# A four-layer graph and attention kernel: a reordered prologue and an earlier first choice

## What is computed

```python
h = (x @ W.T).reshape(n, H, D)                       # the values
e_l = einsum('nhd,hd->nh', h, a_l); e_r = einsum('nhd,hd->nh', h, a_r)
logits = leaky_relu(e_l[:, None] + e_r[None, :], 0.2) + gate * einsum('ijf,hf->ijh', abs(curv_i - curv_j), Wc)
out = einsum('ijh,jhd->ihd', softmax(where(adj > 0, logits, -1e9), axis=1), h)
...
q = x @ Wq_pk; sim = q . pk_keys                     # 2 x 128 scores for each row and head
the 16 best of each half, their 256 sums, the 16 best of those: 16 rows of a table of 131072
k, v = softmax(scores) . keys_table[rows], values_table[rows]
out = causal attention of x @ Wq with k and v, @ Wo
```

## Time and profile before

| what | value |
|---|---|
| time, median of 3 executions | 4347.53 us (4346.95 to 4349.38) |
| profiled execution, its own time | 4337.04 us |
| span of the profiled execution | 4335.3 us |
| mean granted TensorE clock | 0.918 |
| busy: PE, DVE, ACT, POOL | 80%, 77%, 53%, 47% |

### The profile page before, as it was taken

One profiled execution on the slowest core, in us unless ns is written; L12 is line 12 of the kernel. 1 busy time (PEld: TensorE's weight loads), 2 busy tenths in 40 slices (PEclk: granted clock), 3 DMA queues, 4 the chain that ended last, 5 costly groups with the idle time before them and its releaser, 6 DMA issues. The chain is left out here.

```text
span 4335.3 us, 62381 instructions
## 1 busy us (share of the span) xinstructions
PE 3470.9 (80%) x19465; PEld 2679.8 (62%) x19592; DVE 3336.2 (77%) x10591; ACT 2284.3 (53%) x3657; POOL 2049.0 (47%) x2052
## 2 busy tenths in 40 slices
PE   6867777777778788888888989566888888888797
PEld 4645555555555565566666666445677777777575
DVE  2679889899898898898988989663877777777334
ACT  5645455555555555565555655222656666665232
POOL 0377777777777777777766767660000000000000
PEclk9988889999999999999999999777999999999799
DMA  2244444554555555555555556554000000000100
GB/s 75 61 128 118 133 139 134 146 153 141 156 149 162 168 170 174 170 179 176 180 180 184 189 168 205 171 181 160 1 1 1 1 1 1 1 1 1 41 0 10
DMA packets 187672, 477.90 MB, mean 110 GB/s; under 512 B 43933, under 2 KB 87137, under 8 KB 182881
## 3 DMA queue, kind: packets, MB, share of 16 engines
q0 software_dynamic: 98304, 268.57, 21.4%
q1 hardware_dynamic: 89052, 205.52, 14.0%
HBM read 447.57 MB, written 26.21 MB: 109 GB/s over the span
## 5 line engine op out<-in xcount | busy, mean ns | idle before, releaser
L508 POOL DMA_INDIRECT ck_ring<-in_tables,ck_rows x2048 | 2048.8, 1000 | 879.4 <-issue 751.3
L993 DVE SCALAR_TENSOR_TENSOR ck_part<-ck_ring,ck_norm_w,ck_part 128x256 f32<-128x256 f32 x1792 | 768.7, 475 | 62.5 <-DVE ck_rows L968 41.7
L567 PE MATMUL psV<-ck_vals,ck_probsT 128*128 128x128 f32 x4096 | 554.2, 284 | 112.3 <-ACT ck_probsT L742 105.8
L552 PE MATMUL psL<-ck_bias_rhs,ck_bias_w 110*128 110x512 f32 x1024 | 571.7, 641 | 87.0 <-ACT ck_bias_rhs L729 38.4
L567 PEld LDWEIGHTS psV<-ck_vals,ck_probsT 128*128 128x128 f32 x4096 | 501.8, 196 | 161.3 <-ACT ck_probsT L742 92.0
L1204 PE MATMUL psL<-ga_probsT,ga_vals 128*128 128x256 f32 x2048 | 528.1, 405 | 0.7 <-ACT ga_probsT L1301 0.7
L742 ACT COPY ck_probsT<-psT 128x512 f32<-128x512 f32 x512 | 281.3, 587 | 443.5 <-PE psT L559 439.1
L1204 PEld LDWEIGHTS psL<-ga_probsT,ga_vals 128*128 128x128 f32 x2048 | 398.7, 205 | 51.6 <-ACT ga_probsT L1301 0.9
L1191 PE MATMUL psT<-ident,ga_probs 128*128 128x128 f32 x2048 | 303.0, 283 | 153.8 <-ACT ga_probsT L1301 149.5
L1191 PEld LDWEIGHTS psT<-ident,ga_probs 128*128 128x128 f32 x2048 | 248.8, 146 | 204.4 <-issue 184.1
L1292 ACT ACTIVATE ga_probs<-ga_probs,ga_neg_mx 128x2048 f32<-128x2048 f32 x128 | 256.5, 2004 | 220.9 <-DVE ga_neg_mx L1352 220.5
(11 more groups left out here) (205 smaller groups left out, 5616.0 us busy)
## 6 DMA issues: line engine op xcount, KB each, us to landing
ck_ring<-in_tables,ck_rows POOLq DMA_INDIRECT x2048
ck_adj_raw<-in_adj SPq DMA_DIRECT2D x16, 1024.0 KB, 9.5
adj_scratch<-ck_adj_neg SPq DMA_DIRECT2D x16, 512.0 KB
values_scratch<-ck_values_tile SPq DMA_DIRECT2D x128, 64.0 KB, 1.7
keysT_scratch<-ck_keys_tile SPq DMA_DIRECT2D x128, 64.0 KB
ck_keysT<-keysT_scratch SPq DMA_DIRECT2D x8, 1024.0 KB
ck_values<-values_scratch SPq DMA_DIRECT2D x8, 1024.0 KB
ga_adj_neg<-adj_scratch SPq DMA_DIRECT2D x16, 512.0 KB, 11.9
```

The costliest lines, as they stand in the source:

```text
L508: pool.indirect_dma_start(ring[:, slot, :], None, ins["tables"], bass.IndirectOffsetOnAxis(rows[:, k, s:s + 1], axis=0)).then_inc(got[(u * ...
L552: last = nc.tensor.matmul(psL[:, c * CH:(c + 1) * CH], bias_w[:, :], bias_rhs[:, k % 2, c * CH:(c + 1) * CH], start=False, stop=True)
L567: last = nc.tensor.matmul(psV[:, k % 2, :], probsT[:, q % 2, s, :], vals[:, j, :], start=(j == 0), stop=(j == T - 1))
L993: done.append(c.did(nc.vector.scalar_tensor_tensor(part[:, s % 2, :], ring[:, slot, :], norm_w[:, s:s + 1], part[:, s % 2, :], ALU.mult, A ...
```

## The change

There are two parts, all in the one stage. In the prologue, SP issues the loads of L445 to L454 before it waits, and the wait for the right scores and the two transfers of them come last; its constant goes from 13 to 12. TensorE multiplies left and right scores before the values are multiplied the second time, and ScalarE copies in the same order, with the first difference put between the second and third copy of the values. VectorE makes the first mask before it picks the left scores. In the first unit with a choice (`opening`), the scores go ahead of the next logits on TensorE, their copy ahead of relu and difference on ScalarE, and the choice ahead of the next maximum on VectorE.

```diff
@@ SP
-                sp.wait_ge(prep_copied, 13)
-                for b in range(2):
-                    sp.dma_start(bias_rhs[KW:KB, b, :], er_rows[0:H, :]).then_inc(er8_in, 16)
                 sp.dma_start(wq[:, :, :], ins["Wq_pk"]).then_inc(keys_in, 16)
...
                 sp.dma_start(ahead[:, :], ins["c_ahead"][:, 0, 0:P]).then_inc(at_in, 16)
+                sp.wait_ge(prep_copied, 12)
+                for b in range(2):
+                    sp.dma_start(bias_rhs[KW:KB, b, :], er_rows[0:H, :]).then_inc(er8_in, 16)
@@ TensorE, prologue
+                pe.wait_ge(weights_ready, 2)
+                pe.wait_ge(prep_copied, 4)
+                for c in range(NC):
+                    nc.tensor.matmul(psL[...], al_w, hT[...], start=True, stop=True).then_inc(prep_mm, 1)
+                for c in range(NC):
+                    pe.wait_ge(prep_copied, 5 + c)
+                    nc.tensor.matmul(psL[...], ar_w, hT[...], start=True, stop=True).then_inc(prep_mm, 1)
                 for q in range(4):
-                    pe.wait_ge(prep_copied, 4 + q)
+                    if q >= 2:
+                        pe.wait_ge(prep_copied, 11 + q)
...
-                pe.wait_ge(weights_ready, 2)
-                pe.wait_ge(prep_copied, 8)
...
@@ TensorE, tile
-                        if s1:
+                        opening = choosing and not adding and k == 0
+                        if s1 and not opening:
                             if k < KU - 1:
                                 logits_of(t, k + 1)
...
                             nc.tensor.matmul(psT[:, 1, 0:2 * NK], qT[:, :], keys[:, k, :],
                                              start=True, stop=True).then_inc(sim_done, 1)
+                        if opening:
+                            logits_of(t, k + 1)
@@ ScalarE, prologue (behind the copies of hT)
+                for c in range(NC):
+                    act.wait_ge(prep_mm, 4 + c + 1)
+                    nc.scalar.mul(el_wide[...], psL[...], 1.0 - SLOPE).then_inc(prep_copied, 1)
+                act.wait_ge(prep_mm, 12)
+                nc.scalar.copy(er_rows[:, :], psL[:, :]).then_inc(prep_copied, 4)
                 for q in range(4):
-                    act.wait_ge(prep_mm, 4 + q + 1)
+                    act.wait_ge(prep_mm, 12 + q + 1)
                     nc.scalar.copy(vals[...], psT[:, q % 2, :]).then_inc(prep_copied, 1)
+                    if q == 1:
+                        act.wait_ge(cols_ready, 1)
+                        nc.scalar.activation(bias_rhs[0:KC, 0, :], c_rows[:, :], ACT.Relu, bias=c_cols[:, 0:1]
+                                             ).then_inc(diff_ready, 1)
...
                 act.wait_ge(cols_ready, 2)
-                act.wait_ge(prep_copied, 16)
+                act.wait_ge(prep_copied, 12)
@@ ScalarE, tile, and ahead of the loop
+                        opening = choosing and t == 1 and k == 0
+                        if opening:
+                            act.wait_ge(sim_done, v + 1)
+                            act.wait_ge(sim_free, v + 1)
+                            nc.scalar.copy(sim[...], psT[:, 1, 0:2 * NK]).then_inc(sim_copied, 1)
                         if s1 and ahead:
                             relu_of(t, k + 1)
...
-                        if choosing:
+                        if choosing and not opening:
...
-                diff_of(0, 0)
@@ VectorE, prologue
                 dve.wait_ge(consts_in, 16 * (G + 8))
-                dve.wait_ge(prep_copied, 12)
-                nc.vector.tensor_tensor(el_wide..., node_pick..., ALU.mult).then_inc(el_mult, 1)
-                dve.wait_ge(el_mult, 1)
-                nc.vector.tensor_reduce(el_cols[:, :], el_wide..., ALU.add).then_inc(cols_ready, 1)
                 nc.vector.tensor_scalar(c_cols[:, :], c_cols[:, :], -1.0, None, ALU.mult).then_inc(cols_ready, 1)
...
                 turn_adj(0)
+                dve.wait_ge(prep_copied, 8)
+                nc.vector.tensor_tensor(el_wide..., node_pick..., ALU.mult).then_inc(el_mult, 1)
+                dve.wait_ge(el_mult, 1)
+                nc.vector.tensor_reduce(el_cols[:, :], el_wide..., ALU.add).then_inc(cols_ready, 1)
                 dve.wait_ge(keys_in, 64)
@@ VectorE, tile
-                        if s1 and ahead:
+                        opening = choosing and not adding and k == 0
+                        if s1 and ahead and not opening:
                             max_of(t + (k + 1) // KU, (k + 1) % KU)
...
                             attend_now()
+                        if opening:
+                            max_of(t, k + 1)
```

More of the change, by code:

```diff
@@ L519, in _ @@
                                      start=True, stop=True).then_inc(prep_mm, 1)
+                pe.wait_ge(weights_ready, 2)
+                pe.wait_ge(prep_copied, 4)
+                for c in range(NC):
+                    nc.tensor.matmul(psL[:, c * CH:(c + 1) * CH], al_w, hT[:, c * CH:(c + 1) * CH],
+                                     start=True, stop=True).then_inc(prep_mm, 1)
+                for c in range(NC):
+                    pe.wait_ge(prep_copied, 5 + c)
+                    nc.tensor.matmul(psL[:, c * CH:(c + 1) * CH], ar_w, hT[:, c * CH:(c + 1) * CH],
+                                     start=True, stop=True).then_inc(prep_mm, 1)
                 for q in range(4):
-                    pe.wait_ge(prep_copied, 4 + q)
+                    if q >= 2:
+                        pe.wait_ge(prep_copied, 11 + q)
                     for s in range(4):
@@ L526, in _ @@
                     last.then_inc(prep_mm, 1)
-                pe.wait_ge(weights_ready, 2)
-                pe.wait_ge(prep_copied, 8)
-                for c in range(NC):
-                    nc.tensor.matmul(psL[:, c * CH:(c + 1) * CH], al_w, hT[:, c * CH:(c + 1) * CH],
-                                     start=True, stop=True).then_inc(prep_mm, 1)
-                for c in range(NC):
-                    pe.wait_ge(prep_copied, 9 + c)
-                    nc.tensor.matmul(psL[:, c * CH:(c + 1) * CH], ar_w, hT[:, c * CH:(c + 1) * CH],
-                                     start=True, stop=True).then_inc(prep_mm, 1)
                 def logits_of(t, k, first=False):
@@ L704, in _ @@
                     nc.scalar.copy(hT[:, c * CH:(c + 1) * CH], psL[:, c * CH:(c + 1) * CH]).then_inc(prep_copied, 1)
+                for c in range(NC):
+                    act.wait_ge(prep_mm, 4 + c + 1)
+                    nc.scalar.mul(el_wide[:, c * CH:(c + 1) * CH], psL[:, c * CH:(c + 1) * CH],
+                                  1.0 - SLOPE).then_inc(prep_copied, 1)
+                act.wait_ge(prep_mm, 12)
+                nc.scalar.copy(er_rows[:, :], psL[:, :]).then_inc(prep_copied, 4)
                 for q in range(4):
-                    act.wait_ge(prep_mm, 4 + q + 1)
+                    act.wait_ge(prep_mm, 12 + q + 1)
                     nc.scalar.copy(vals[:, 4 * q:4 * q + 4, :].rearrange("p s c -> p (s c)"),
                                    psT[:, q % 2, :]).then_inc(prep_copied, 1)
-                for c in range(NC):
-                    act.wait_ge(prep_mm, 8 + c + 1)
-                    nc.scalar.mul(el_wide[:, c * CH:(c + 1) * CH], psL[:, c * CH:(c + 1) * CH],
-                                  1.0 - SLOPE).then_inc(prep_copied, 1)
-                act.wait_ge(prep_mm, 16)
-                nc.scalar.copy(er_rows[:, :], psL[:, :]).then_inc(prep_copied, 4)
+                    if q == 1:
+                        act.wait_ge(cols_ready, 1)
+                        nc.scalar.activation(bias_rhs[0:KC, 0, :], c_rows[:, :], ACT.Relu, bias=c_cols[:, 0:1]
+                                             ).then_inc(diff_ready, 1)
                 act.wait_ge(cols_ready, 2)
-                act.wait_ge(prep_copied, 16)
+                act.wait_ge(prep_copied, 12)
                 def relu_of(t, k):
@@ L776, in tile @@
                             nc.scalar.copy(qT[:, :], psT[:, 0, 0:P]).then_inc(qT_copied, 1)
+                        opening = choosing and t == 1 and k == 0
+                        if opening:
+                            act.wait_ge(sim_done, v + 1)
+                            act.wait_ge(sim_free, v + 1)
+                            nc.scalar.copy(sim[:, k % 2, :, :].rearrange("p a b -> p (a b)"),
+                                           psT[:, 1, 0:2 * NK]).then_inc(sim_copied, 1)
                         if s1 and ahead:
@@ L1063, in _ @@
                 turn_adj(0)
+                dve.wait_ge(prep_copied, 8)
+                nc.vector.tensor_tensor(el_wide.rearrange("p (u i) -> p u i", i=G),
+                                        el_wide.rearrange("p (u i) -> p u i", i=G),
+                                        node_pick[:, :].unsqueeze(1).to_broadcast([P, UNITS, G]),
+                                        ALU.mult).then_inc(el_mult, 1)
+                dve.wait_ge(el_mult, 1)
+                nc.vector.tensor_reduce(el_cols[:, :], el_wide.rearrange("p (u i) -> p u i", i=G),
```

(1 more changed line is left out.)

6 lines of the change are left out of this document (removed).

## The result

The changed kernel takes 4322.41 us (median of 4, 4321.4 to 4325.73) against 4347.92 us: a ratio of 0.9942, with a 95% interval of 0.9925 to 0.996, or 25.5 us less. I had forecast 4330.7, with a range down to 4323.5, so the sign was right and the size was beyond the range. The two profiled executions tell another number: 4337.04 us before and 4321.98 after, which is 15.1. Much of what follows is about why these differ.

What follows compares the result with a forecast made beforehand. Late loads behind the right scores bound the prologue, then gathers set the pace to about 1000 us, VectorE after. 11.4 (prologue) + 5.4 (first choice) = 16.8 us off, forecasting 4330.7 us from the median; range 4323.5 to 4339.6.

Steps and rivals of the forecast that it cites:

- The chain of the prologue: Prologue: left scores start 7.4 us earlier, right scores' copy ends at 32.1, and everything later gains what the first maximum gains.
- The loads: Prologue, SP's queue: loads and right scores' transfers open TensorE's gate at 41.5 instead of 52.9, 11.4 us earlier.
- 29.3 + 9.4 = 38.7: Prologue: loads land at 38.7, needing 9.4 us after the transfer engines are busy until 29.3.
- 42.2: Prologue: gate time if the right scores' transfers queue 3.5 us behind the loads, on the same few engines.
- The first choice: First unit with a choice: choice and first gather 5.4 us earlier, with the lead kept.
- The cost on the other engines: First unit with a choice: 0.3 us lost on the chain of VectorE, ScalarE and TensorE.
- From profile to median: Whole kernel: median lies 10.5 us above the profiled execution, so 4320.2 becomes 4330.7.
- The lost lead: Rival 1, after the first choice: the gathers' lead is lost, giving 4336.4; chance 0.15.
- loads that get in their own way: Rival 3, prologue: right scores wait behind 2 MB, gate opens near 50, giving 4339.2 to 4345; chance 0.05.
- The quicker transfers: Rival 2, prologue: gate opens at 36.6 to 38, first logits at full clock, giving 4324.3; chance 0.15.
- The fourth rival: Boundaries: idle TensorE at half clock costs 2.3 us at each of 15 boundaries, giving 4365; chance 0.03.
- The signs I had named: Profile after: left scores 23.0, gate near 42, first maximum near 48.8, gather waits about 5 us shorter, later boundaries 16.8 earlier.

Runs made afterwards that it cites:

- the changed kernel delayed: Changed kernel plus three useless memsets on VectorE ahead of its first maximum; 4333.2 us.
- the kernels kept warm: Useless TensorE matmuls added at boundaries: kernel before 4308.2 us, changed kernel 4286.1, prologue alone 4292.1, first choice alone 4301.2.
- the kernel with SP's order alone: Kernel before with only SP's order changed: loads first, then the wait and the right scores' transfers; 4339.4 us, ratio 0.9984.

## Why the prediction was off

**The chain of the prologue: right.** Left and right scores follow directly, SP waits last, the gate is the right scores' transfer, and the first maximum comes out of it. The copies end 5.3 us earlier in the pair of profiles, at 34.2 instead of the 32.1 forecast, since the first matmuls ran at half clock for longer in this execution; where they did not (the changed kernel delayed), they end at 32.2. That all that follows gains what the first maximum gains was nearly right: 13.4 of 14.2 us at the end of the tile.

**The loads: wrong in size.** The step of the prologue that failed is what comes behind "29.3 + 9.4 = 38.7": right scores that need "3.5 us more", taken together as a gate at 41.5, 2.8 us behind the loads. The landing itself came near: `ahead` was in at 37.9, and between 37.0 and 39.8 over seven profiles. Luck had a part in that. The nine microseconds had been read from a stretch in which 1.5 MB of the next mask moved along (284 GB/s from 42 to 54), and I had the loads start on engines that are busy until 29.3; in fact the queue took loads and constants together, at 216 GB/s from 21 on. Behind the landing the gate took 1.8 us in this profile and 1.3 to 2.4 in the seven, not 2.8. So the term was 11.4 us and measured 14.2 in the pair of profiles: 1.8 from the gate (39.7; 0.8 of it by the landing, 1.0 by what follows it), 0.2 since the gate of before was at 53.15 and not at 52.9, and 0.8 from the clock, which rose 3 us after the first logits began instead of 4.5. (The 6.5 us that I called half speed are so only in their first 4.5: the last matmul in the earlier trace rows takes 1.02.) The means of five profiles each, above, give 15.0, and the medians of the kernels kept warm 16.1, or 14.3 by their ratios. The Trainium skill's rule (DMA: Bandwidth & Descriptors, "Why a DMA increments its semaphore by 16 and not by 1") splits a transfer over the largest number of engines, up to 16, that divides its slowest dimension, and on a queue like SP's takes the lowest-numbered ones. As I read it, few engines would carry tail and scores one after another, which would have made 42.2. No row here shows the engines apart (the share of 0.30 that I called six of 16 is nearer five). The gates, 39.4 to 41.6, are all earlier than that, though they do follow the end of the loads.

**The first choice: right, a little small.** 5.1 and 5.4 us earlier for the gather in two profiles (5.4 forecast), kept up to the last tile in the kernels kept warm, as argued from the 12.0 us of waits. The cost on the other engines was mis-sized: not 0.3 but 1.6 us (the third unit's maximum), since the next logits, a unit's worth of waiting later, ran in part at half clock (1.92 us at 139.72), and VectorE waited 4.1 us for a relu. It did not matter, as the gathers set the pace: they and their quicker mean made 6.1 to 6.5 us in the profiles, 7.0 kept warm (6.1 by the ratios).

**From profile to median: the other step that failed.** "The median of the runs lies 10.5 us above it, and I take the difference from that" treats the offset as fixed. It was not: the profile of before lay in the lower heap, that of the changed kernel on its own median, 0.4 us from it. Right would have been the effect of the change with several microseconds of uncertainty for the clock in both directions. By the kernels kept warm the sum is 22.1 us (20.0 by the ratios) and not 16.8; with it the forecast would have been 4325.4 to 4327.5, inside the range. The measured 25.5 has 3 to 5 us more, which put the time just outside it. That they belong to where the clock fell in the executions of the kernel before fits its two profiles (3.4 us of their 7.7 in the fourteen boundaries, 1.2 in the prologue, 3.2 behind the last tile), but was not shown for the executions that make the median.

**The rivals.** The lost lead (0.15) and loads that get in their own way (0.05) did not come. The quicker transfers (0.15), with 4324.3, came nearest in the number, by luck: the right scores landed at 39.7 and not by 38, and the clock did not stay up. The fourth rival, with the price of 2.3 us for each boundary whose logits run at half clock, named a mechanism that in fact moves this kernel's time, by a chance of 0.03 and only as a loss; against it I had written that a shift by 5 us leaves the waits as they are. The delay of 2.9 us speaks against that: single boundaries became up to 3.4 us longer and 2.5 shorter.

**The signs I had named.** The gate's releaser, the half clock of the first logits and the gather's lead were as listed; the gate (39.7 for 42) and the first maximum (46.1 for 48.8) came earlier than listed, the left scores (25.2 for 23.0) later, and the waits for gathers shrank by 7 us instead of 5. "Each boundary 16.8 us earlier than before" was wrong from the third tile on (20 to 21 us, falling to 15), and "if the shift changes between 200 and 2900 us" is what made the sum fail, though for another reason than a lost lead.

## What to carry to other kernels

Before the gain of a change is taken from one profile, ask whether the profile lies in the same heap as the median, and profile the old kernel twice: here its two profiles were 8 us apart, half as much as the forecast change. Where TensorE waits a few microseconds at every boundary of a loop, the length of what follows depends on the clock; matmuls of no use in those waits took 38 and 36 us from the two kernels, more than the change itself, and made the boundaries of different kernels the same to 0.8 us. A small transfer that is issued behind large loads on the same queue came in 1.3 to 2.4 us behind the last of them, whether it was issued at 32 or at 34 us; to forecast it, forecast the landing of what is ahead of it, and then the time of its own issue matters little.

## What the hardware showed that I had not expected

- TensorE did its first matmuls at half clock (weight loads of 0.34 us instead of 0.19) until somewhere between 21.8 and 23.7 us in eleven of fourteen profiles, and at full clock from the start in three, although the profile gives the granted clock as 1.00 there.
- A boundary took 28.3 or 30.5 us with nearly the same waits of TensorE (3.22 and about 1.9 us), by where in it the clock fell, and 26.6 us where the waits were filled.
- On one of the three chips the executions of the same kernel before fell into two heaps some 12 us apart (about 4339 and 4352), those of the changed kernel within 6 us (4319.4 to 4325.7). Between profiles the boundaries' clock moves the sum by up to 10 us; that it makes the heaps is argued from this and not shown, and what puts one execution into the one or the other was not tried.
- An issue on SP's queue took up to 3.7 us where the queue was full (the attention's weights in the kernel with SP's order alone; 0.6 us in the kernel before).
- Right scores that were issued at 32.2 and at 34.3 us, behind the same loads, opened the gate at 39.9 and 39.7.
